# Four indirect gathers on their way at most, and weighing tile by tile, in the last three passes of a graph network

## The chip, the cores and the metric

One Trainium2 chip, and of it one core. The metric is the device time of the program in microseconds: the median of three runs. Times of single instructions, here and later, come from one execution that the hardware profiler recorded.

## The reference

Four layers of a graph network run one after the other over the same graph of 12,500 nodes with 48 features and 212,500 edges, sorted by their target node. Each layer reads the source node's row of every edge, scales it, and adds it up at the edge's target (or, in the second layer, the other way round). The third and fourth layers are what the change concerns:

```
h = relu(layernorm(x));  ex = exp(e - segment_max(e)[dst]);  a = ex / segment_sum(ex)[dst]
x = x + elu(segment_sum(h[src] * a, dst))
h = relu(layernorm(x))
y1 = segment_sum(h[src] * w, dst);  y2 = segment_sum(y1[src] * w, dst)
x = x + (h + y1 + y2) / 3
```

That makes three light passes over all edges: one for the third layer (49 columns, the last of them a column of ones that yields the sum of the weights), and two for the fourth (48 columns each).

## The kernel before

The edges are cut into tiles of 128 (one edge a partition), four tiles to a group (G = 4), eight groups to a turn of the loops (GB = 8). There are 416 groups, 52 turns and 1,664 tiles in a pass. The target nodes are cut into blocks of 128. Since the edges are sorted by target, a group touches one block or two; each block that it touches is a window.

`light_pass` (lines 718 to 822) is called three times, as `l2`, `l3a` and `l3b`, with `order` 0, 1 and 2. Its engines work so:

- **ScalarE** writes the row indices of a group as integers into a slot of `idx` (`stage`, line 743). It stages six groups ahead (LEAD = 6) of eight slots. Before it stages the group six ahead it waits for VectorE's `s_done` (line 750). Then it waits until the group's gathers have landed (line 754), and multiplies each of the four tiles by its edge weights, in place in `ring` (line 756). The fourth of these raises `s_weighed`.
- **GpSimd** waits for the group's indices (line 734) and issues four indirect gathers of 128 rows each from DRAM into `ring` (line 736). Nothing else holds it back. All four raise the group's own semaphore of eight, `s_landed_rows[j]`, by 16 each.
- **TensorE** waits for `s_weighed`, and in each window multiplies the four tiles with one-hot matrices (`hot`) and adds them up in one of two banks of `psum_acc` (line 816).
- **VectorE** makes the one-hot matrices of a window by one compare over 128 x 512 elements (line 789, two inputs in SBUF: `iota` and `dstf`). Behind it, it adds the bank of the window before to the sum of its block (`keep`, line 778). So the compare of a group's window comes behind the `keep` of the window two before it. A group's second window uses the same `hot` buffer as its first, so its compare waits until TensorE has finished the first.

The first layer (`first_pass`, its gathers in line 504) and the second (scatter-adds in line 1097) are not changed. In the second, each scatter waits on GpSimd for the scatter four before it to have landed (line 1094 to 1096, K = 4 semaphores in turn), which is the form that the change brings to the gathers.

Two semaphore habits are of use in reading the code. `sem_inc(s_seen, 1)` after a wait binds the wait to an instruction of the sequencer's own; it is one instruction with the wait. A landed DMA raises its semaphore by 16.

Of the kernel before, what the change touches and what calls it, by code (L numbers as in the profile page):

```python
# [16 lines left out]
G = 4  # L17
RING = 4
GB = 2 * RING
# [3 lines left out]
TURNS = NG // GB  # L23
# [4 lines left out]
DEPTH = GB  # L28
# [21 lines left out]
def gnn_kernel(nc, x, dst_cols, src_cols, dst_rows, src_rows, w_cols, logit_cols, logit_rows,  # L50
# [10 lines left out]
    with ExitStack() as ctx:  # L61
        def sb(name, shape, dt=f32):
            return ctx.enter_context(nc.sbuf_tensor(name, shape, dt))

        def sem(name):
            return ctx.enter_context(nc.semaphore(name))
# [41 lines left out]
        idx = sb("idx", [P, DEPTH * G], i32)  # L108
# [46 lines left out]
        ring = tbl_flat[:, 0:DEPTH * G * CS].rearrange("p (s c) -> p s c", c=CS)  # L155
# [304 lines left out]
        s_maxed = sem("s_maxed")  # L460
        s_closed = sem("s_closed")
        s_seen = sem("s_seen")
        s_landed_rows = [sem(f"s_landed_rows{j}") for j in range(DEPTH)]
        s_spread = sem("s_spread")
        s_picked = sem("s_picked")
        s_kept = sem("s_kept")
# [8 lines left out]
        def load_ranges(eng, i):  # L475

            regs = range_regs[eng]
            eng.load(regs, ranges[0:1, ds(i * (2 * GB), 2 * GB)])
            return [(eng.snap(regs[2 * j], min_val=0, max_val=NB - 1), eng.snap(regs[2 * j + 1], min_val=1, max_val=NB))
                    for j in range(GB)]  # L480
# [239 lines left out]
        def light_pass(order, name, src_table, cols, weights, total, before=None):  # L720
            s_idx = sem(name + "_idx")
            s_done = sem(name + "_done")
            s_clear = sem(name + "_clear")
            s_weighed = sem(name + "_weighed")
            s_flushed = sem(name + "_flushed")
            arrived = order * TURNS * 16 * G

            with nc.Block() as block:
                @block.gpsimd
                def _(pool):  # L730
                    with pool.Fori(0, TURNS) as i:
                        for j in range(GB):
                            pool.wait_ge(s_idx, i * GB + (j + 1))
                            pool.sem_inc(s_seen, 1)
                            for u in range(j * G, (j + 1) * G):
                                pool.indirect_dma_start(  # L736
                                    out=ring[:, u, 0:cols], out_offset=None, in_=src_table,
                                    in_offset=bass.IndirectOffsetOnAxis(ap=idx[:, u:u + 1], axis=0)).then_inc(s_landed_rows[j], 16)

                @block.scalar  # L740
                def _(act):
                    def stage(slot, column):
                        nc.scalar.copy(idx[:, slot * G:(slot + 1) * G], srow[:, ds(column, G)]).then_inc(s_idx, 1)  # L743

                    for j in range(LEAD):
                        stage(j, j * G)
                    with act.Fori(0, TURNS) as i:
                        for j in range(GB):
                            act.wait_ge(s_done, i * GB + (j + 1))
                            act.sem_inc(s_seen, 1)  # L750
                            stage((j + LEAD) % DEPTH, i * U + (j + LEAD) * G)

                            act.wait_ge(s_landed_rows[j], i * (16 * G) + (arrived + 16 * G))
                            act.sem_inc(s_seen, 1)
                            for u in range(G):
                                last = nc.scalar.activation(ring[:, j * G + u, 0:cols], ring[:, j * G + u, 0:cols], ACT.Copy,  # L756
                                                            scale=weights[:, ds(i * U + (j * G + u), 1)])
                            last.then_inc(s_weighed, 1)

                @block.vector  # L760
                def _(dve):
                    if before is not None:
                        before(dve)
                    nv.memset(acc_flat, 0.0).then_inc(s_clear, 1)
                    nv.memset(psum_acc[:, :, 0:CS], 0.0).then_inc(s_clear, 1)
                    dve.wait_ge(s_clear, 2)
                    dve.sem_inc(s_done, 1)
                    if order == 0:
                        dve.sem_inc(s_kept, 1)
                        dve.reg_mov(wn_dve, 1)  # L770
                    dve.reg_mov(before_dve, NB)

                    def keep(win, s_made):
                        k = dve.snap(before_dve, min_val=0, max_val=NB)
                        block_acc = total[:, ds(k, 1), 0:cols].rearrange("p b c -> p (b c)")
                        dve.wait_ge(s_kept, win)
                        dve.wait_ge(s_picked, win + 1)
                        nv.tensor_tensor(block_acc, block_acc,  # L778
                                         psum_acc[:, ds((win + 1) & 1, 1), 0:cols].rearrange("p r c -> p (r c)"), ALU.add).then_inc(s_made, 1)

                    with dve.Fori(0, TURNS) as i:
                        spans = load_ranges(dve, i)
                        for j in range(GB):
                            dve.reg_mov(room_dve, dve.snap(wn_dve))
                            with dve.Fori(*spans[j]) as k:
                                win = dve.snap(wn_dve)
                                dve.wait_ge(s_picked, dve.snap(room_dve))
                                dve.sem_inc(s_seen, 1)
                                nv.tensor_tensor(hot[:, j % 2, :, :],  # L789
                                                 iota[:, ds(k * P, P)].unsqueeze(1).to_broadcast([P, G, P]),  # L790
                                                 dstf[:, ds(i * U + j * G, G)].unsqueeze(2).to_broadcast([P, G, P]),
                                                 ALU.is_equal).then_inc(s_spread, 1)
                                keep(win, s_kept)
                                dve.reg_mov(before_dve, k)
                                dve.reg_add(wn_dve, wn_dve, 1)
                                dve.reg_add(room_dve, wn_dve, 1)
                            dve.sem_inc(s_done, 1)  # L797
                    keep(dve.snap(wn_dve), s_flushed)

                @block.tensor  # L800
                def _(pe):
                    if order == 0:
                        pe.sem_inc(s_picked, 2)
                        pe.reg_mov(wn_pe, 1)
                    with pe.Fori(0, TURNS) as i:
                        spans = load_ranges(pe, i)
                        for j in range(GB):
                            pe.wait_ge(s_weighed, i * GB + (j + 1))
                            pe.sem_inc(s_seen, 1)
                            with pe.Fori(*spans[j]) as k:  # L810
                                win = pe.snap(wn_pe)
                                pe.wait_ge(s_kept, win)
                                pe.sem_inc(s_seen, 1)
                                pe.wait_ge(s_spread, win)
                                for u in range(G):
                                    last = nc.tensor.matmul(psum_acc[:, ds(win & 1, 1), 0:cols].rearrange("p r c -> p (r c)"),  # L816
                                                            hot[:, j % 2, u, :], ring[:, j * G + u, 0:cols],
                                                            start=(u == 0), stop=(u == G - 1))
                                last.then_inc(s_picked, 1)
                                pe.reg_add(wn_pe, wn_pe, 1)  # L820
# [358 lines left out]


        light_pass(0, "l2", table2, CS, lg, acc)

        s_var3 = sem("s_var3"); s_std3 = sem("s_std3"); s_centred3 = sem("s_centred3"); s_squared3 = sem("s_squared3")
# [38 lines left out]
        third = 1.0 / (LAYERS + 1)  # L1222
        y1 = acc_flat[:, 0:NBW * C].rearrange("p (b c) -> p b c", c=C)
        light_pass(1, "l3a", table3[0], C, w, y1)
        s_y1out = sem("s_y1out")
        with nc.Block() as block:
# [69 lines left out]
```

## Time and profile before

| | us |
|---|---|
| median of three runs | 12057.81 |
| lowest and highest | 12056.52 and 12058.14 |
| span of the profiled execution | 14556.0 |
| GpSimd busy in that span | 9189.0 |
| TensorE matmuls busy | 6194.2 |
| VectorE busy | 4412.4 |
| ScalarE busy | 3916.7 |

The profiled execution is 2,498 us longer than the median of the runs without the profiler. Of the profiled execution no own device time is given beside its span, so the span stands for it. In the profile the light passes start at 6645.8, 9321.2 and 11919.7 us. A line of the views gives an engine, the line of the kernel, the operation, the tiles written and read, and how often it came; "idle before" is how long the engine stood still ahead of it and what ended that. DMA_INDIRECT under POOL is the time in which GpSimd makes the descriptors of a gather or a scatter, not the time in which data moves.

### The profile page before, as it was taken

The page shows a single profiled execution, that of the slowest core. Times are in us where ns is not written, and L with a number is a line of the kernel's source. Part 1 is how long each engine was busy: PE and PEld are TensorE (multiplying, and loading weights), DVE is VectorE, ACT ScalarE, POOL GpSimd, SP SyncE. Part 2 cuts the span into 40 slices and gives each one's busy share as a digit, 9 for nine tenths or more (in the row PEclk, how much of TensorE's full clock was granted, in tenths as well). Part 3 has the DMA queues.
Part 4 walks back from the last instruction along what each step waited for, and adds up shares of the span by engine and source line. Part 5 has one row for each costly group of instructions (what it writes and reads, how often), then busy time and mean ns, then how long its engine had stood idle before and what let it go on. Part 6 is the DMA issues. An engine that isn't in the chain of part 4 may idle for free. (4 is left out here: it accounts for less than half of the span.)

```text
span 14556.0 us, 229228 instructions
## 1 busy us (share of the span) xinstructions
PE 6194.2 (43%) x41742; PEld 4831.3 (33%) x41743; DVE 4412.4 (30%) x18474; ACT 3916.7 (27%) x13496; POOL 9189.0 (63%) x8348
## 2 busy tenths in 40 slices
PE   4444444444555555552333333333333333333333
PEld 2222222223444444442333333233333333333333
DVE  4444444445444444443111111211111111111111
ACT  3444444443333333321111111111121111111111
POOL 5555555556888888884666666566666656666665
DMA  4333333334455554541111111111111111111111
GB/s 116 100 102 102 99 97 96 96 94 63 61 62 61 61 62 61 62 59 42 16 16 16 16 16 16 20 16 16 16 16 16 16 21 16 16 16 16 16 16 21
DMA packets 805020, 671.18 MB, mean 46 GB/s; under 512 B 417876, under 2 KB 663828, under 8 KB 802727
## 3 DMA queue, kind: packets, MB, share of 16 engines
q0 software_dynamic: 452736, 234.14, 14.8%
q1 hardware_dynamic: 349659, 430.53, 11.2%
q10 hardware_dynamic: 2588, 6.12, 0.1%
q14 instruction: 26, 0.21, 0.0%
q8 instruction: 11, 0.18, 0.0%
HBM read 562.94 MB, written 107.13 MB: 46 GB/s over the span
## 5 line engine op out<-in xcount | busy, mean ns | idle before, releaser
L736 POOL DMA_INDIRECT table<-table,idx x4992 | 4838.7, 969 | 3149.9 <-ACT idx L743 1638.0
L816 PE MATMUL psum_acc<-table 128*128 128x48 f32 (+1 forms) x12288 | 2946.7, 417 | 5074.1 <-DVE acc L778 2363.5
L816 PEld LDWEIGHTS psum_acc<-table 128*128 128x128 f32 x12288 | 2733.0, 328 | 5287.7 <-issue 5244.2
L1097 POOL DMA_INDIRECT sums<-rows,idx x1664 | 2619.5, 1574 | 577.6 <-issue 430.9
L504 POOL DMA_INDIRECT rows<-table,idx x1668 | 1670.2, 1001 | 1581.9 <-ACT idx L556 1059.2
L789 DVE TENSOR_TENSOR table<-iota,dstf 128x512 f32 x1536 | 1064.6, 693 | 3059.2 <-issue 2074.7
L743 ACT CAST idx<-srow 128x4 int32 (+1 forms) x1266 | 243.2, 193 | 6322.7 <-DVEq L797 4262.1
L778 DVE TENSOR_TENSOR acc<-acc,psum_acc x1539 | 311.3, 202 | 3420.0 <-remote 2352.8
L704 PE MATMUL psum_acc<-parts,onehot 128*128 128x48 bf16 x6144 | 338.8, 215 | 1600.5 <-DVE onehot L647 1433.7
L1013 PE MATMUL psum_exp<-table,onet 128*128 x6144 | 432.3, 219 | 1376.2 <-DVE onet L932 1166.2
L756 ACT ACTIVATE table<-table,w 128x48 f32<-128x48 f32 x3328 | 840.6, 323 | 26.2 <-DMA table<-table,idx 12.4
L1013 PEld LDWEIGHTS psum_exp<-table,onet 128*128 128x128 bf16 x6144 | 341.8, 116 | 1510.4 <-issue 1487.5
L704 PEld LDWEIGHTS psum_acc<-parts,onehot 128*128 128x128 bf16 x6144 | 271.8, 117 | 1686.8 <-DVE onehot L647 1500.9
L986 PE MATMUL psum_mlp<-w2s,hid 49*128 49x48 f32 x3336 | 808.3, 414 | 50.8 <-DMA hid<-hid_dram 50.7
L986 PEld LDWEIGHTS psum_mlp<-w2s,hid 49*128 49x128 f32 x3336 | 741.2, 324 | 124.5 <-issue 124.5
L597 ACT ACTIVATE scratch<-drow,far 128x512 f32<-128x512 uint16 x512 | 369.3, 721 | 598.8 <-DVE segmax L666 293.2
L1064 ACT ACTIVATE gate<-psum_mlp,adapt,cw 128x48 f32<-128x48 f32 x1664 | 514.1, 390 | 48.8 <-issue 26.2
L1043 ACT CAST parts<-rest 128x196 bf16<-128x196 f32 x416 | 149.9, 360 | 1281.1 <-DVE rest L913 903.8
L964 DVE TENSOR_TENSOR idx<-srow,dmp 128x4 int32<-128x4 f32 x416 | 67.9, 163 | 1321.3 <-POOLq L1099 1243.8
L691 PE MATMUL psum_mlp<-srcrow,w1s 40*48 40x512 f32 x416 | 396.9, 1056 | 153.3 <-issue 152.2
L573 ACT ACTIVATE prod<-rows,w 128x48 f32<-128x48 f32 x1668 | 426.0, 324 | 54.0 <-issue 39.9
L756 ACT ACTIVATE table<-table,lg 128x49 f32<-128x49 f32 x1664 | 422.0, 325 | 14.2 <-DMA table<-table,idx 9.1
(183 smaller groups left out, 7162.2 us busy)
## 6 DMA issues: line engine op xcount, KB each, us to landing
drow<-rows_dram SPq DMA_DIRECT2D x832, 128.0 KB
lrow<-in_logit_rows SPq DMA_DIRECT2D x416, 256.0 KB
table<-table,idx POOLq DMA_INDIRECT x4992
srcrow<-rows_dram SPq DMA_DIRECT2D x416, 128.0 KB
hid_dram<-hid SPq DMA_DIRECT2D x416, 96.0 KB
hid<-hid_dram SPq DMA_DIRECT2D x416, 96.0 KB
rows<-table,idx POOLq DMA_INDIRECT x1668
sums<-rows,idx POOLq DMA_INDIRECT x1664
```

Of the source, the lines that this page charges most:

```text
L504: pool.indirect_dma_start(out=rows[:, u, 0:width], out_offset=None, in_=src_table, in_offset=bass.IndirectOffsetOnAxis(ap=idx[:, u:u + 1], ...
L573: last = nc.scalar.activation(prod[:, j % 2, u, 0:cols], rows[:, j % RING * G + u, 0:cols], ACT.Copy, scale=weights[:, ds(i * U + (j * G + ...
L691: nc.tensor.matmul(psum_mlp[j % 2][0:C, :], w1s[:, :], attr[j % 2], start=True, stop=True).then_inc(s_mlp1, 1)
L704: last = nc.tensor.matmul(psum_acc[:, 0, 0:cols], onehot[:, u, :], parts[:, j % 2, u, q, 0:cols], start=(u == 0 and q == 0), stop=(u == G ...
L736: pool.indirect_dma_start(out=ring[:, u, 0:cols], out_offset=None, in_=src_table, in_offset=bass.IndirectOffsetOnAxis(ap=idx[:, u:u + 1], ...
L756: last = nc.scalar.activation(ring[:, j * G + u, 0:cols], ring[:, j * G + u, 0:cols], ACT.Copy, scale=weights[:, ds(i * U + (j * G + u), 1)])
L789: nv.tensor_tensor(hot[:, j % 2, :, :], iota[:, ds(k * P, P)].unsqueeze(1).to_broadcast([P, G, P]), dstf[:, ds(i * U + j * G, G)].unsqueez ...
L816: last = nc.tensor.matmul(psum_acc[:, ds(win & 1, 1), 0:cols].rearrange("p r c -> p (r c)"), hot[:, j % 2, u, :], ring[:, j * G + u, 0:col ...
L986: last = nc.tensor.matmul(psum_mlp[j % 2][:, u * C:(u + 1) * C], hid[:, j % 2, u * P:(u + 1) * P], w2s[:, :], start=True, stop=True)
L1013: last = nc.tensor.matmul(psum_exp[j % 2][:, u * CT:(u + 1) * CT], onet[:, u * P:(u + 1) * P], table[:, ds(k, 1), q, :].rearrange("p b c - ...
L1064: last = nc.scalar.activation(gate[:, j % 2, u, 0:C], psum_mlp[j % 2][:, u * C:(u + 1) * C], ACT.Identity, scale=cw[:, ds(t, 1)], bias=ada ...
L1097: pool.indirect_dma_start(out=sums[c], out_offset=bass.IndirectOffsetOnAxis(ap=idx[:, slot:slot + 1], axis=0), in_=rows[:, slot, 0:CS], in ...
```

## The change

In the light passes there are four landing semaphores in place of eight, one for each tile of a group. GpSimd waits ahead of each gather until the gather of the same tile in the group before has landed, so that at most four gathers are on their way. In the very first turn of the first light pass the first four gathers have nothing to wait for, so that turn is written out ahead of the loop. ScalarE waits for each tile by itself instead of for the whole group.

```
-        s_landed_rows = [sem(f"s_landed_rows{j}") for j in range(DEPTH)]
+        s_landed_rows = [sem(f"s_landed_rows{u}") for u in range(G)]
...
-            arrived = order * TURNS * 16 * G
+            arrived = order * TURNS * 16 * GB
...
-                    with pool.Fori(0, TURNS) as i:
+                    def turn(i, peeled):
                         for j in range(GB):
                             pool.wait_ge(s_idx, i * GB + (j + 1))
                             pool.sem_inc(s_seen, 1)
-                            for u in range(j * G, (j + 1) * G):
+                            for u in range(G):
+                                if j > 0 or not peeled:
+                                    pool.wait_ge(s_landed_rows[u], i * (16 * GB) + (arrived + 16 * j))
+                                    pool.sem_inc(s_seen, 1)
                                 pool.indirect_dma_start(
-                                    out=ring[:, u, 0:cols], out_offset=None, in_=src_table,
-                                    in_offset=bass.IndirectOffsetOnAxis(ap=idx[:, u:u + 1], axis=0)).then_inc(s_landed_rows[j], 16)
+                                    out=ring[:, j * G + u, 0:cols], out_offset=None, in_=src_table,
+                                    in_offset=bass.IndirectOffsetOnAxis(ap=idx[:, j * G + u:j * G + u + 1], axis=0)).then_inc(s_landed_rows[u], 16)
+
+                    if order == 0:
+                        turn(0, True)
+                        with pool.Fori(1, TURNS) as i:
+                            turn(i, False)
+                    else:
+                        with pool.Fori(0, TURNS) as i:
+                            turn(i, False)
...
-                            act.wait_ge(s_landed_rows[j], i * (16 * G) + (arrived + 16 * G))
-                            act.sem_inc(s_seen, 1)
                             for u in range(G):
+                                act.wait_ge(s_landed_rows[u], i * (16 * GB) + (arrived + 16 * (j + 1)))
+                                act.sem_inc(s_seen, 1)
                                 last = nc.scalar.activation(ring[:, j * G + u, 0:cols], ring[:, j * G + u, 0:cols], ACT.Copy,
                                                             scale=weights[:, ds(i * U + (j * G + u), 1)])
                             last.then_inc(s_weighed, 1)
```

## Rows read from the trace of the kernel before

**Rows 1.** Whole execution, groups by line, engine, operation: busy, mean ns, idle before, releaser.

```profile
L736 POOL DMA_INDIRECT table<-table,idx x4992 | 4838.7, 969 | 3149.9 <-ACT idx L743 1638.0 <-issue 1511.9
L1097 POOL DMA_INDIRECT sums<-rows,idx x1664 | 2619.5, 1574 | 577.6 <-issue 430.9 <-ACT rows L1050 76.8 <-DMA sums<-rows,idx 42.6
L504 POOL DMA_INDIRECT rows<-table,idx x1668 | 1670.2, 1001 | 1581.9 <-ACT idx L556 1059.2 <-issue 522.6
```

**Rows 2.** Who waited for whom, whole execution: total us, times, longest us.

```profile
POOL table L736 <- ACT idx L743: 1638.0, 292, 103.7
```

**Rows 3.** Timeline (start, duration, engine, work): GpSimd's first gather of the later two passes.

```profile
9321.24 0.94 POOL L736 DMA_INDIRECT table<-table,idx  x1 [69.00 <-ACT idx L743]
...
11919.66 4.91 POOL L736 DMA_INDIRECT table<-table,idx  x1 [23.55 <-ACT idx L743]
```

**Rows 4.** Third light pass, groups by line.

```profile
L789 DVE TENSOR_TENSOR table<-iota,dstf 128x512 f32 x512 | 355.1, 694 | 1073.4 <-issue 746.1 <-remote 275.8 <-PE psum_acc L816 51.5
L743 ACT CAST idx<-srow 128x4 int32 x416 | 80.4, 193 | 2114.6 <-DVEq L797 1462.8 <-issue 500.2 <-remote 136.5
L756 ACT ACTIVATE table<-table,w 128x48 f32<-128x48 f32 x1664 | 420.3, 323 | 8.5 <-DMA table<-table,idx 3.3
```

**Rows 5.** Timeline: gathers one after the other.

```profile
8003.52 0.94 POOL L736 DMA_INDIRECT table<-table,idx  x1 [0.31 <-issue]
...
8012.26 0.95 POOL L736 DMA_INDIRECT table<-table,idx  x1 [0.30 <-issue]
```

**Rows 6.** Timeline at the start of the first light pass.

```profile
6649.61 0.94 POOL L736 DMA_INDIRECT table<-table,idx  x1 [0.30 <-issue]
6652.23 1.02 ACT L756 ACTIVATE table<-table,lg 128x49 f32<-128x49 f32 x4 [1.70 <-DMA table<-table,idx]
...
6657.32 1.01 ACT L756 ACTIVATE table<-table,lg 128x49 f32<-128x49 f32 x4 [3.49 <-DMA table<-table,idx]
...
6659.05 1.93 PE L816 MATMUL psum_acc<-table 128*128 128x49 f32 x8 [2.97 <-issue]
6659.70 0.95 POOL L736 DMA_INDIRECT table<-table,idx  x1 [0.30 <-issue]
...
6662.36 1.01 ACT L756 ACTIVATE table<-table,lg 128x49 f32<-128x49 f32 x4 [3.94 <-DMA table<-table,idx]
```

**Rows 7.** Timeline in the second layer: scatters, each behind a wait for an earlier one.

```profile
5002.37 1.56 POOL L1097 DMA_INDIRECT sums<-rows,idx  x1 [0.30 <-issue]
5004.23 1.56 POOL L1097 DMA_INDIRECT sums<-rows,idx  x1 [0.30 <-issue]
```

**Rows 8.** Timeline of the first light pass: compares, sums, matmuls and gathers.

```profile
8022.77 0.69 DVE L789 TENSOR_TENSOR table<-iota,dstf 128x512 f32 x1 [0.61 <-issue]
8023.38 0.20 DVE L778 TENSOR_TENSOR acc<-acc,psum_acc  x1
8023.66 0.19 ACT L743 CAST idx<-srow 128x4 int32 x1 [8.61 <-DVEq L797]
...
8023.70 3.82 PE L816 MATMUL psum_acc<-table 128*128 128x49 f32 x16 [5.99 <-DVE acc L778]
8023.85 1.01 ACT L756 ACTIVATE table<-table,lg 128x49 f32<-128x49 f32 x4
8024.16 0.69 DVE L789 TENSOR_TENSOR table<-iota,dstf 128x512 f32 x1 [0.59 <-issue]
8024.64 1.03 POOL L736 DMA_INDIRECT table<-table,idx  x1 [5.04 <-ACT idx L743]
8025.96 0.21 DVE L778 TENSOR_TENSOR acc<-acc,psum_acc  x1 [1.10 <-PE psum_acc L816]
...
8026.88 0.69 DVE L789 TENSOR_TENSOR table<-iota,dstf 128x512 f32 x1 [0.71 <-issue]
8027.22 1.17 POOL L736 DMA_INDIRECT table<-table,idx  x1 [0.30 <-issue]
8027.84 0.21 DVE L778 TENSOR_TENSOR acc<-acc,psum_acc  x1 [0.27 <-PE psum_acc L816]
```

**Rows 9.** Timeline: a compare in the middle of a gather, and one just ahead of one.

```profile
8035.01 0.94 POOL L736 DMA_INDIRECT table<-table,idx  x1 [0.30 <-issue]
8035.41 0.69 DVE L789 TENSOR_TENSOR table<-iota,dstf 128x512 f32 x1 [3.90 <-issue]
...
9154.35 0.69 DVE L789 TENSOR_TENSOR table<-iota,dstf 128x512 f32 x1 [8.62 <-issue]
9154.40 1.46 POOL L736 DMA_INDIRECT table<-table,idx  x1 [0.30 <-issue]
```

**Rows 10.** Timeline: a second window's compare behind its first window's matmuls.

```profile
7132.68 1.94 PE L816 MATMUL psum_acc<-table 128*128 128x49 f32 x8 [7.00 <-DVE table L789]
...
7134.90 0.69 DVE L789 TENSOR_TENSOR table<-iota,dstf 128x512 f32 x1 [2.35 <-PE psum_acc L816]
```

## The prediction

> **What bounds the kernel now.** I read the groups by line first [rows 1]. GpSimd does one thing in each of the three parts, and its busy time is the making of descriptors: 944 ns is the usual gather (the timeline has 0.94 almost everywhere) [rows 5], 969 ns the mean in the light passes. Between two gathers it stands still for 0.30 us, which the trace calls issue. From 8003.52 to 8012.26 there are seven gathers in 8.74 us, a period P of 1.249 us [rows 5].
>
> Then I asked how much of the profiled span is left when GpSimd never waits for indices. It waits 1,059.2 us in the first layer and 1,638.0 in the light passes [rows 1]. Of the latter, 103.7 and 69.0 and 23.6 us are the openings of the three passes, where a table is first written [rows 2, 3], and stay. 14,556.0 - 1,059.2 - 1,638.0 + 103.7 + 69.0 + 23.6 = 12,055 us. The median of the runs is 12,057.8. So I read the profiled execution as the real one plus some 2,500 us of index waits. What ends them is VectorE's late `s_done`, which VectorE's sequencer raises late (the compare and the sum idle for "issue" and "remote") [rows 4], and without the profiler this seems to be nearly absent. The real kernel then is bound by GpSimd through all its length: a light pass is 1,664 gathers x 1.249 = 2,078 us plus whatever lengthens single gathers. All terms below are worked out for such an undisturbed light pass and added to 12,058.
>
> **The wait ahead of each gather.** It adds 4,988 waits and as many small register operations on GpSimd. Queued behind each is the gather itself, and behind that all further gathers and the next group's index wait; ScalarE waits for them. Two things must be known. First, when it is met: ScalarE starts to weigh 2.62 and 2.66 us after the start of the group's last gather [rows 6], its own start-up within. The gather four later starts at 4 P = 5.00 us. Second, how much ahead GpSimd must be released: after the end of an index write it needs 24.64 - 23.85 = 0.79 us to start a gather [rows 8]. 5.00 - 2.66 - 0.79 leaves 1.55 us. So the limit of four is never reached: at the start of a gather two or three are on their way. The nearest row for the same form is the scatter, with a wait ahead of each: the gap stays 0.30 [rows 7]. There the wait for an earlier scatter does end 42.6 us of idle time in 1,664 [rows 1]; for 4,992 gathers that would be 128 us, the upper bound. Below zero nothing can come of it, since nothing competes for what fewer gathers would free. I take 0, nearest to the 0.30 row, and the 1.55 us is the cover: if landing took 4.2 us in place of 2.66, each further 0.1 us would cost 0.1 us a group, 125 us in all. The turn that is written out once costs nothing I can name.
>
> **The waits of ScalarE.** Three more waits and value computations a group. The present one costs nothing visible: index write until 23.85, weighing from 23.85 [rows 8]. ScalarE has 0.19 + 1.01 us of work in a group of 5.00 us. At 0 to 0.1 us each, they are hidden, all but that of the fourth tile, which was there before as the group's.
>
> **What tile by tile moves.** Tiles 0 to 2 are weighed while later ones are being gathered. Behind the last landing stands one multiply of 0.33 us instead of four in 1.01 us. Everything behind it, TensorE and VectorE, comes 0.68 us earlier against GpSimd's beat. At the end of a pass that is a gain of 0.68 us, 2 us for three. In the middle no one waits for it. It has a side effect, though, and this is what I rest the forecast on.
>
> **The compare holds up the gather.** A gather that starts while a compare runs takes longer. Compare 9154.35, gather 9154.40: 1.46 us instead of 0.94. Compare 0.34 us ahead: 1.17. Compare 0.48 us ahead: 1.03. A compare that starts 0.40 us into a gather: 0.94 [rows 8, 9]. All lie on one line: the gather is longer by 0.565 us less the compare's lead, for leads from about 0.05 to 0.565, and otherwise not at all. The sum (line 778), with one of its two inputs in PSUM, shows no such effect. 126 us of the light passes' 4,838.7 are of this kind (4,838.7 - 4,992 x 0.944), 8 of them two gathers at the third pass's opening, the first of 4.91 us [rows 3].
>
> The Trainium skill (SBUF — State Buffer, Who interferes with whom) says that a two-input VectorE instruction takes the read side of a shared port pair against GpSimd, and infers that this leaves descriptor making alone. The rows say otherwise, at least for the read of the indices at its start. By the page's inference the side effect would be nil and the time 12,056.
>
> So the question is where the compares fall in the beat. With s the start of a group's last gather:
> - A regular compare: 2.66 to the weighing, 1.01 the four multiplies, 0.72 to the first matmul (6658.33 to 6659.05) [rows 6], 1.93 the matmuls, 0.32 to the sum (8027.52 to 8027.84) and 0.92 from sum to compare (8025.96 to 8026.88) [rows 8]: s + 7.56. The sixth gather after s starts at 7.49. The compare comes 0.07 after it: harmless. With the change: s + 6.88, between the fifth (6.24) and the sixth, 0.61 ahead of this: harmless, by 0.05 us.
> - A pass has 512 compares for 416 groups [rows 4], so 96 groups have a second window (taken as two at most). Its compare waits for the first window's matmuls: 0.28 us here [rows 10], 0.32 to the sum [rows 8]; I take 0.36, with the register operations that the sum lacks. s + 6.68; before, 0.44 after the fifth gather, harmless. With the change s + 6.00, 0.24 ahead of it: 0.32 us.
> - The compare behind it follows at 1.39 (8022.77 to 8024.16). Before: 8.07, 0.58 after the sixth, harmless. Changed: 7.39, and the sixth now starts at 7.49 + 0.32, a lead of 0.42: 0.14 us.
> - The third follows the second window's matmuls: 0.92 + 1.93 + 0.32 + 0.92 = 4.09 after the first. Before: 10.77, a lead of 0.47 on the ninth gather at 11.24: 0.10 us. Changed: 10.09, lead 0.36 on the eighth at 9.99 + 0.46: 0.20 us.
>
> Before 0.10, changed 0.66 us, for 96 groups and three passes: 29 and 190 us, a difference of 161.
>
> These leads hang on hundredths. The whole chain may be shorter or longer without the profiler by an unknown e, the same for both kernels. At e = -0.1 and +0.1 the same arithmetic gives about 165 and 180. At -0.2 the regular compares of before lead by 0.13 and cost some 0.17 us each (a delay pushes the next lead down, so less than half of the 0.43 remains), and the difference falls to about 23. At +0.2 the second-window compare of the changed kernel no longer leads, and the changed kernel gains some 48. Landings scatter too and smear this. The mean of these five is 96; less 2 for the pass ends that is 94, and the forecast is 12,058 + 94 = 12,152 us, 0.8% slower.
>
> **The rivals.**
> - No measurable change. The phases smear out so that both kernels pay alike, or the queue of ready gathers hides what the compare takes. For it: ScalarE, TensorE and VectorE are off the bound, and the limit does not bind. Against it: the gather is the bound, so that each lengthening counts in full. Time 12,056.
> - Faster. The place is the same, the fifth to ninth gather after a landing, and the price the same, but before pays: if the real chain is 0.2 us or more longer, or 0.15 to 0.4 shorter with little damping, its compares lead and the changed ones do not. It decides at a regular lead above 0.05 us before. For it: 12,055 above includes the traced 126 us of such lengthening, room for before to be paying. Against: most of those in the trace follow a restart of GpSimd after an index wait (8024.64), which the real run lacks. Gain 48 to 126: about 11,985.
> - The landing wait binds after all: 128 us by the scatter's row, 12,186.
>
> **How the numbers follow.** Forecast 0.42, no change 0.25, faster 0.27, landing wait 0.06. What can be told from no change is about 0.2%, 24 us. Slower than that: 0.46 (a little of the forecast's own spread falls below 24); within: 0.27; faster: 0.27. The forecast's own range is 12,080 to 12,250 (23 to 192 more). To 8 in 10 it must take in no change and the nearer part of faster: 12,000 to 12,250.
>
> **What would show it.** In the changed profile: 0.30 us ahead of gathers and no "DMA" among the releasers of line 736's successor (the wait is never late); single multiplies in step with the gathers at a pass start, and the first matmul about 0.7 us sooner after the last landing; the mean gather above 969 ns if the forecast holds, and many gathers of 1.1 to 1.3 us in undisturbed stretches. I am wrong if an effect stays with the group-wise wait of ScalarE restored, or if removing the second input's conflict from the compare changes nothing.

## The result, and the profile after

The changed kernel takes 12,187.5 us (median of four runs, 12,185.2 to 12,189.7) against 12,057.2 before: 130 us more, ratio 1.0108 with a 95% interval of 1.0094 to 1.0123. The forecast was 12,152 us, with a range of 12,000 to 12,250.

The profiled execution of the changed kernel has a span of 12,183.5 us, as long as its runs. That of before had 14,556.0 and was 2,500 us too long. So its trace is no fair partner, and the kernel before was profiled again (label `r1_before_again`, below): span 12,053.8, as long as its runs. From here on "before" in comparisons is that trace.

GpSimd's groups by line, with busy time, mean ns of one, and idle time ahead and its releasers, first of the changed kernel, then of the kernel before in its new trace. They answer to [rows 1]. "Gaps" below means the idle time between two gathers.

```profile
L739 POOL DMA_INDIRECT table<-table,idx x4992 | 4898.2, 981 | 1732.1 <-DMA table<-table,idx 1299.1 <-issue 253.5 <-ACT idx L754 179.6
L1108 POOL DMA_INDIRECT sums<-rows,idx x1664 | 2620.9, 1575 | 577.8 <-issue 434.6 <-ACT rows L1061 73.5 <-DMA sums<-rows,idx 44.1
L504 POOL DMA_INDIRECT rows<-table,idx x1668 | 1697.2, 1018 | 546.5 <-issue 474.6 <-ACT idx L556 71.8
```

```profile
L736 POOL DMA_INDIRECT table<-table,idx x4992 | 4804.7, 962 | 1699.4 <-issue 1511.5 <-ACT idx L743 187.9
L1097 POOL DMA_INDIRECT sums<-rows,idx x1664 | 2621.4, 1575 | 577.1 <-issue 442.1 <-ACT rows L1050 72.9 <-DMA sums<-rows,idx 36.5
L504 POOL DMA_INDIRECT rows<-table,idx x1668 | 1693.6, 1015 | 546.5 <-issue 478.8 <-ACT idx L556 67.7
```

The whole difference of the spans, 129.7 us, is in these rows. The gathers of the light passes take 4,898.2 - 4,804.7 = 93.5 us more, the gaps between them 1,732.1 - 1,699.4 = 32.7 more, the first layer's gathers (unchanged code) 3.6 more, the scatters 0.2. The index waits of the old trace (1,059.2 and 1,638.0 in [rows 1]) are 67.7 and 187.9 here, most of the latter the openings of the passes.

One name misleads. The changed kernel's 1,299.1 us "DMA" are 4,264 gaps of 0.30 us, the ordinary gap that is called "issue" before: where a gather has a wait ahead of it, the profile names the wait's releaser for the gap, even when it was met long before.

The longer gathers are seen in a timeline of the changed kernel, around a group with a second window (start, duration, engine, work):

```profile
8003.63 0.94 POOL L739 DMA_INDIRECT table<-table,idx  x1 [0.30 <-issue]
8004.57 0.69 DVE L800 TENSOR_TENSOR table<-iota,dstf 128x512 f32 x1 [4.86 <-PE psum_acc L827]
8004.88 1.20 POOL L739 DMA_INDIRECT table<-table,idx  x1 [0.30 <-DMA table<-table,idx]
...
8005.96 0.69 DVE L800 TENSOR_TENSOR table<-iota,dstf 128x512 f32 x1 [0.59 <-issue]
8006.38 1.09 POOL L739 DMA_INDIRECT table<-table,idx  x1 [0.30 <-DMA table<-table,idx]
...
8008.68 0.69 DVE L800 TENSOR_TENSOR table<-iota,dstf 128x512 f32 x1 [0.72 <-issue]
8009.02 1.17 POOL L739 DMA_INDIRECT table<-table,idx  x1 [0.30 <-DMA table<-table,idx]
```

Three compares lead a gather by 0.31, 0.42 and 0.34 us, and the gathers are 0.26, 0.15 and 0.23 us longer than 0.94: each 0.565 less the lead. The same place before, again with the compares of a second window and of the group behind it:

```profile
8001.94 0.94 POOL L736 DMA_INDIRECT table<-table,idx  x1 [0.30 <-issue]
8002.26 0.69 DVE L789 TENSOR_TENSOR table<-iota,dstf 128x512 f32 x1 [4.76 <-PE psum_acc L816]
...
8003.19 0.94 POOL L736 DMA_INDIRECT table<-table,idx  x1 [0.30 <-issue]
...
8003.66 0.69 DVE L789 TENSOR_TENSOR table<-iota,dstf 128x512 f32 x1 [0.59 <-issue]
8004.43 0.94 POOL L736 DMA_INDIRECT table<-table,idx  x1 [0.30 <-issue]
...
8013.10 0.69 DVE L789 TENSOR_TENSOR table<-iota,dstf 128x512 f32 x1 [0.72 <-issue]
8013.17 1.45 POOL L736 DMA_INDIRECT table<-table,idx  x1 [0.30 <-issue]
```

The first two compares start 0.32 and 0.47 us after a gather's start and cost nothing. But the last pair shows what before does pay: a regular compare (one of a group's first window) which comes 0.07 us ahead of a gather, and costs 0.51.

The longer gaps stand ahead of every 110th gather of the changed kernel, 45 times, 0.8 to 1.25 us instead of 0.30:

```profile
5783.19 0.94 POOL L739 DMA_INDIRECT table<-table,idx  x1 [0.31 <-issue]
5785.09 0.95 POOL L739 DMA_INDIRECT table<-table,idx  x1 [0.95 <-issue]
...
5925.56 0.95 POOL L739 DMA_INDIRECT table<-table,idx  x1 [0.30 <-issue]
5927.70 0.94 POOL L739 DMA_INDIRECT table<-table,idx  x1 [1.19 <-issue]
```

### The profile page after: what moved, and what is told of

It reads as the page before. It is cut to its first block and busy times, and to the rows that moved or that the text cites. A ratio compares the mean times of both kernels' runs of the same rounds, so it can differ in the third digit from the quotient of the medians.

```text
span 12183.5 us, 240282 instructions
## 1 busy us (share of the span) xinstructions
PE 6218.6 (51%) x41742; PEld 4831.6 (40%) x41743; DVE 4451.5 (37%) x18474; ACT 4143.7 (34%) x13496; POOL 9277.1 (76%) x8348
## 5 line engine op out<-in xcount | busy, mean ns | idle before, releaser
L739 POOL DMA_INDIRECT table<-table,idx x4992 | 4898.2, 981 | 1732.1 <-DMA table<-table,idx 1299.1
L504 POOL DMA_INDIRECT rows<-table,idx x1668 | 1697.2, 1018 | 546.5 <-issue 474.6
L767 ACT ACTIVATE table<-table,w 128x48 f32<-128x48 f32 x3328 | 1050.0, 332 | 2055.8 <-DMA table<-table,idx 2030.0
L767 ACT ACTIVATE table<-table,lg 128x49 f32<-128x49 f32 x1664 | 526.9, 333 | 1028.0 <-DMA table<-table,idx 1015.1
```

The source lines that it names most:

```text
L504: pool.indirect_dma_start(out=rows[:, u, 0:width], out_offset=None, in_=src_table, in_offset=bass.IndirectOffsetOnAxis(ap=idx[:, u:u + 1], ...
L739: pool.indirect_dma_start(out=ring[:, j * G + u, 0:cols], out_offset=None, in_=src_table, in_offset=bass.IndirectOffsetOnAxis(ap=idx[:, j ...
```

## Experiments

The theory: waiting tile by tile moves VectorE's compares into the way of the gathers. The rivals: the limit of four, or the waits themselves, cost the time, and no VectorE instruction matters. Where a ratio is given, it is against the kernel before.

**The kernel before once more, for its profile.** No edit.

> The kernel before, unchanged, to get a profile of it that is as long as its runs. The profile that the prediction rests on was 2,498 us longer than the runs; that of the changed kernel is not. Theory (compares hold up gathers): span near 12,056; the light-pass gathers take in sum 4,712 us plus 30 to 60 (mean 950 to 956 ns) against 4,898 (mean 981) in the changed kernel, so that their difference alone gives 130 us. Rival (landing wait): the gathers sum to the same 4,898 and the difference stands in the gaps between them.

Measured: 12,057.4 us, ratio 0.9998 (0.9987 to 1.0008), gathers 4,804.7 us, mean 962. The direction is as the theory has it, but the gathers of before are longer by 93 us than 4,712, not by 30 to 60. Their difference gives 94 of the 130 us, not all. The other 33 are in the gaps: so both the theory and a rival have a part.

**Limit of four, ScalarE waits for the whole group.**

```
                             for u in range(G):
                                 act.wait_ge(s_landed_rows[u], i * (16 * GB) + (arrived + 16 * (j + 1)))
                                 act.sem_inc(s_seen, 1)
+                            for u in range(G):
                                 last = nc.scalar.activation(...)
```

> The changed kernel with its limit of four gathers and its wait ahead of each on GpSimd, but ScalarE waits for all four tiles before it weighs the first. Theory (tile by tile moves the compares by 0.68 us into the gathers' path): back to the kernel before, 12,057, ratio 1.000 within 0.002. Rival (landing wait or the added instructions on GpSimd): stays at 12,187, ratio 1.011.

Measured: 12,099.9 us, ratio 1.0034 (1.0022 to 1.0047). Two thirds of the loss go, one third stays. The prediction had named this as a sign of being wrong: "an effect stays with the group-wise wait of ScalarE restored". One does, 43 us. The gathers are back, the gaps are not:

```profile
L739 POOL DMA_INDIRECT table<-table,idx x4992 | 4810.9, 964 | 1735.2 <-DMA table<-table,idx 1294.2 <-ACT idx L754 290.7 <-issue 150.3
```

**Limit of eight, tile by tile.**

```
-        s_landed_rows = [sem(f"s_landed_rows{u}") for u in range(G)]
+        s_landed_rows = [sem(f"s_landed_rows{u}") for u in range(2 * G)]
...
-            arrived = order * TURNS * 16 * GB
+            arrived = order * TURNS * 16 * (GB // 2)
...
-                                if j > 0 or not peeled:
-                                    pool.wait_ge(s_landed_rows[u], i * (16 * GB) + (arrived + 16 * j))
+                                v = j % 2 * G + u
+                                if j > 1 or not peeled:
+                                    pool.wait_ge(s_landed_rows[v], i * (8 * GB) + (arrived + 16 * (j // 2)))
```

(and `v` in the gather and in ScalarE's wait likewise)

> The changed kernel with eight landing semaphores and a limit of eight gathers; ScalarE still waits tile by tile. Theory: as the changed kernel, 12,187, ratio 1.011. Rival (a limit of four is tight): back towards 12,057.

Measured: 12,131.9 us, ratio 1.0062 (1.0045 to 1.0079). Neither expectation is met: the limit is worth some 55 us against the changed kernel by the medians, 43 by the spans of the two profiled executions, and 33 by their gaps. The gaps are back, the gathers are not:

```profile
L740 POOL DMA_INDIRECT table<-table,idx x4992 | 4889.4, 979 | 1699.0 <-DMA table<-table,idx 1378.2 <-ACT idx L755 178.8 <-issue 142.0
```

**The changed kernel with another compare.**

```
-                                nv.tensor_tensor(hot[:, j % 2, :, :],
-                                                 iota[:, ds(k * P, P)].unsqueeze(1).to_broadcast([P, G, P]),
-                                                 dstf[:, ds(i * U + j * G, G)].unsqueeze(2).to_broadcast([P, G, P]),
-                                                 ALU.is_equal).then_inc(s_spread, 1)
+                                for u in range(G):
+                                    spread_hot = nv.tensor_scalar(hot[:, j % 2, u, :], iota[:, ds(k * P, P)],
+                                                                  dstf[:, ds(i * U + (j * G + u), 1)], None, ALU.is_equal)
+                                spread_hot.then_inc(s_spread, 1)
```

> The changed kernel with the one-hot compare as four instructions over 128x128 with one SBUF matrix and a scalar column each, in place of one with two SBUF matrices over 128x512. Theory, if the second matrix input is what holds up the gather: all of the 178 us that gathers are longer goes, 12,187 - 178 = about 12,010, below the kernel before, and the light-pass gathers have a mean near 945 ns. Rival 1 (any VectorE instruction that reads SBUF holds it up): stays at 12,100 to 12,200. Rival 2 (landing wait): stays at 12,187 with a mean of 981 ns unchanged or lower but the time not.

Measured: 12,020.9 us, ratio 0.9969 (0.9956 to 0.9981), 166 us below the changed kernel though VectorE works longer: its four instructions cover 0.93 and 1.02 us in the timeline where one took 0.69. The gathers have a mean of 948 ns, and one that a compare leads by 0.77 us while its four parts still run is not longer:

```profile
8002.64 1.02 DVE L801 TENSOR_SCALAR table<-iota,dstf 128x128 f32 x4 [0.73 <-issue]
8003.41 0.94 POOL L739 DMA_INDIRECT table<-table,idx  x1 [0.30 <-DMA table<-table,idx]
```

```profile
L739 POOL DMA_INDIRECT table<-table,idx x4992 | 4732.5, 948 | 1735.6 <-DMA table<-table,idx 1443.9 <-ACT idx L754 185.5 <-issue 106.2
```

So it is the compare in its old form that holds up the gather, and no other VectorE work in these passes does so to speak of. The edit changes two things at once, the second matrix input and the size (four of 128x128 in place of one of 128x512). That the second input is what counts is the likelier reading, since each of the four parts still runs 0.3 us beside the gathers, but no run separates the two.

**Limit of eight, ScalarE waits for the group.** The two edits of above together.

> Limit of eight gathers with a wait ahead of each on GpSimd, ScalarE waits for the whole group. So far the kernel with a limit of four and group waits took 12,100, and its trace has a gap of about 1.0 us instead of 0.30 ahead of every 110th gather, which the limit of eight with tile waits does not have. Theory (the added waits cost nothing; the limit of four exposes a pause of GpSimd's sequencer): 12,057, ratio 1.000 within 0.002, sum of gathers about 4,805. Rival (waits ahead of each gather cost by themselves, whatever the limit): about 12,100.

Measured: 12,060.9 us, ratio 1.0001 (0.9991 to 1.0010). A wait ahead of each gather is free by itself, to within 0.1%.

```profile
L740 POOL DMA_INDIRECT table<-table,idx x4992 | 4810.5, 964 | 1699.8 <-DMA table<-table,idx 1298.2 <-ACT idx L755 273.3 <-issue 128.3
```

**Limit of eight, tile by tile, and a delay.**

```
                                 act.sem_inc(s_seen, 1)
+                                if u == G - 1:
+                                    for _ in range(9):
+                                        act.sem_inc(s_delay, 1)
```

> Limit of eight, ScalarE waits tile by tile, but nine semaphore increments on ScalarE between the last tile's wait and its multiply, some 0.68 us, the time by which tile by tile is earlier. Theory (only the moment of the compares against the gathers counts): falls from 12,132 back to about 12,060 although ScalarE has more to do. Rival (tile-wise waits cost by themselves, on ScalarE or through semaphore traffic): 12,132 or more.

Measured: 12,065.3 us, ratio 1.0005 (0.9995 to 1.0014); without the delay it was 1.0062. The delay puts the last tile's weighing 0.60 us later (median), and this extra work for ScalarE makes the kernel 67 us faster, since the compares fall about where they were before. They lengthen the gathers by 94 us here, by 163 without the delay:

```profile
L741 POOL DMA_INDIRECT table<-table,idx x4992 | 4812.1, 964 | 1699.6 <-DMA table<-table,idx 1314.1 <-ACT idx L756 258.5 <-issue 127.1
```

**The kernel before with the other compare**, in the light passes (the edit above, on the kernel before):

> The kernel before (no limit, group waits), with the light passes' compare as four instructions with one SBUF matrix and a scalar column. Theory: the 97 us by which its gathers are longer than 944 ns fall to about 25, as in the changed kernel with these compares, and nothing else moves: 12,057 - 72 = 11,985, ratio 0.994. Rival (the gain in the changed kernel came from elsewhere): 12,057.

Measured: 11,987.8 us, ratio 0.9942 (0.9929 to 0.9956), as expected.

```profile
L736 POOL DMA_INDIRECT table<-table,idx x4992 | 4733.9, 948 | 1699.4 <-issue 1520.0 <-ACT idx L743 179.3
```

**And in the first layer too.**

```
-                                nv.tensor_tensor(onehot[:, :, :], iota[:, ds(k * P, P)].unsqueeze(1).to_broadcast([P, G, P]),
-                                                 dstf[:, ds(i * U + j * G, G)].unsqueeze(2).to_broadcast([P, G, P]),
-                                                 ALU.is_equal).then_inc(s_hot, 1)
+                                for u in range(G):
+                                    first_hot = nv.tensor_scalar(onehot[:, u, :], iota[:, ds(k * P, P)],
+                                                                 dstf[:, ds(i * U + (j * G + u), 1)], None, ALU.is_equal)
+                                first_hot.then_inc(s_hot, 1)
```

> As before, and the same compare in the first layer too, whose 1,668 gathers have a mean of 1,015 ns, 118 us over 944 each. VectorE is busy there for most of the time, and four instructions take some 1.0 us instead of 0.69. Theory, if that compare is half of what holds up these gathers and VectorE keeps up: 11,985 - 40 to 70 = about 11,930. Rival (VectorE becomes the bound in the first layer): 12,000 or more.

Measured: 11,942.8 us, ratio 0.9904 (0.9889 to 0.9919): 114 us below before by the medians of other runs of it, 117 by those beside it, 245 below the changed kernel, and within what was expected. The first layer's gathers fall from a mean of 1,015 to 995 ns, 28% of their excess over 944. Other VectorE instructions there have two matrix inputs too and may be behind the rest, which was not tested.

```profile
L504 POOL DMA_INDIRECT rows<-table,idx x1668 | 1660.3, 995 | 547.1 <-issue 473.0 <-ACT idx L556 74.0
```

**What the pause goes by.** Limit of four, group waits, and `pool.sem_inc(s_delay, 1)` ahead of every gather.

> Limit of four, group waits on ScalarE, and one semaphore increment more on GpSimd ahead of every gather. The kernel without it takes 12,100 and has a gap of 0.8 to 1.25 us ahead of every 110th gather, 45 in all. Theory A (the pause of GpSimd's sequencer belongs to its stream of instructions): the distance between such gaps changes from 110, to about 80 with a fifth to a quarter more instructions, and with them the time, to about 12,115. Theory B (it belongs to the number of gathers): the distance stays 110 and the time 12,100. Either way the increment itself costs nothing: gaps of 0.30 us elsewhere.

Measured: 12,104.2 us, ratio 1.0036 (1.0017 to 1.0056). The distance stays 110 gathers, and the gaps are 45 in number as before, which is theory B: the pause goes with the number of gathers, not with that of instructions.

```profile
L741 POOL DMA_INDIRECT table<-table,idx x4992 | 4809.0, 963 | 1738.3 <-DMA table<-table,idx 1304.2 <-ACT idx L756 281.9 <-issue 152.2
```

The parts together, in us; "gathers" and "gaps" are GpSimd's busy and idle time of the light passes' line:

| kernel | time | ratio | gathers | gaps |
|---|---|---|---|---|
| before | 12,057 | | 4,804.7 | 1,699.4 |
| limit 8, group | 12,061 | 1.0001 | 4,810.5 | 1,699.8 |
| limit 8, tile, delay | 12,065 | 1.0005 | 4,812.1 | 1,699.6 |
| limit 4, group | 12,100 | 1.0034 | 4,810.9 | 1,735.2 |
| limit 8, tile | 12,132 | 1.0062 | 4,889.4 | 1,699.0 |
| limit 4, tile (the change) | 12,187 | 1.0108 | 4,898.2 | 1,732.1 |

Tile by tile costs 79 to 87 us in gathers at either limit, the limit of four 33 to 35 us in gaps with either wait. The two add up in these sums; of the ratios, 0.34% and 0.62% make 0.96% where 1.08% was measured, a difference within their intervals.

## Why the prediction was right, and where it was not

**GpSimd bounds the kernel: right.** What the kernels differ by in its gathers and gaps is found again in the spans of their profiled executions, to within 9 us.

**The old trace as the real run plus index waits: right in the main, to the microsecond by luck.** The sum of 12,055 us was drawn from it; the new trace's span is 12,053.8. But the same working by parts makes the light passes 43 us longer than in the new trace and the first layer 47 us shorter, and the two cancel.

**The compare holds up the gather, by 0.565 us less its lead: right.** Summed over all compares of the changed kernel's trace with leads of 0.045 to 0.565 us, that line gives 176 us, and the gathers that follow are longer by 177. In the new trace of before both are 87. With the other compare the lengthening goes. Here the Trainium skill (SBUF — State Buffer, Who interferes with whom) infers that such an instruction leaves descriptor making alone; the runs say otherwise, up to 0.52 us a gather, and the measurement decides. Its rule that the order of issue decides who blocks is borne out by the trace in both directions. A compare that starts at least 0.045 us ahead of a gather goes first, and the gather is longer. One that starts from 0.045 us ahead to 0.02 us behind is itself the one that is held up: 129 of the 1,536 compares before take 0.70 to 0.77 us instead of 0.69, all end 0.72 us after the gather's start, and the gather keeps its 0.94:

```profile
5979.69 0.94 POOL L736 DMA_INDIRECT table<-table,idx  x1 [0.30 <-issue]
5979.70 0.72 DVE L789 TENSOR_TENSOR table<-iota,dstf 128x512 f32 x1 [0.71 <-issue]
...
8073.56 0.77 DVE L789 TENSOR_TENSOR table<-iota,dstf 128x512 f32 x1 [0.72 <-issue]
8073.61 0.94 POOL L736 DMA_INDIRECT table<-table,idx  x1 [0.30 <-issue]
```

A compare that starts later within a gather takes its 0.69 us, and the gather its 0.94. So in these traces the two collide about a gather's start only, not over all of its 0.94 us.

**How much earlier tile by tile makes the chain: right.** From a group's last gather to its first matmul the prediction had 4.39 us before and 3.71 with the change. The medians are 4.33 and 3.71, so 0.62 us in place of 0.68.

**Where the compares fall: right for the changed kernel, off for before.** The table sets the traces against the prediction. Each cell has the lead over the next gather in us (predicted, or the measured median; "none" is a lead above 0.565), then the cost in us summed over the three passes. There are 288 compares of each of the first three kinds.

| compare | predicted lead, cost before | measured | predicted lead, cost changed | measured |
|---|---|---|---|---|
| second window's | none, 0 | none, 0 | 0.24, 92 | 0.29, 79 |
| the one behind | none, 0 | none (0.73), 5 | 0.42, 40 | 0.42, 37 |
| the third | 0.47, 29 | 0.53, 15 | 0.36, 58 | 0.35, 46 |
| all others | 0.07 behind, 0 | about the gather's start, 67 | 0.61, 0 | 0.65 to 0.69, 15 |

The first three rows are the step that carried the forecast: 161 us predicted, 141 measured. The last row failed: the prediction had the regular compare 0.07 us after a gather's start in before and called it harmless. In the real run the chain is 0.06 us shorter than the slowed trace had it, the median of these compares is 0.01 us after a gather's start, and the chain scatters, from 4.25 to 4.47 us between its tenth and its ninetieth percentile. Of the compares four groups behind a second window, 44% come 0.045 to 0.565 us ahead of a gather, most of them by less than 0.3, where the price is highest, and they alone make 48 us. In all, before pays 67 us that the prediction did not charge, against 15 in the changed kernel: a term mis-sized by some 50 us. The spread over the unknown e, which took 161 down to 96, made up for it: 93.5 us were measured. That it came so near is in part luck, since the mean of five values of e stood in for a size that the prediction did not know.

**The wait ahead of each gather costs nothing, "the 1.55 us is the cover": this step failed.** The waits are free, but a limit of four is not: 33 us. The prediction says that "the limit of four is never reached". GpSimd's sequencer, which runs ahead of the making of descriptors, reaches it at nearly every gather. In the changed kernel the record of the wait stands 0.02 us behind the landing of the gather four before, at 1,223 of the 1,247 gathers for which the trace tells that landing. The landings do not come late. From the start of a gather to its landing it is

```profile
DMA to landing us min/median/max: 2.3/2.4/6.2
```

and so the wait ends 2.59 us (median) ahead of the start of its own gather. A gather starts as little as 0.78 us after its wait, so that in the ordinary case nothing is lost, as predicted. What was left out is what the sequencer itself does now and then. Once in 110 gathers it leaves no record for 3.2 us, and the gather just ahead of this pause starts 3.43 us after its wait, the same in all 45 cases. That is 0.84 us more than the 2.59, and a gap of 0.5 to 0.95 us beyond the usual 0.30 opens, 34 us in all. With a limit of eight the waits end 7.6 us ahead, and the same pause (3.1 us, then once in 106 gathers) leaves no gap. The scatter's row, used as the upper bound (128 us), covered the cost, but it was read as landing waits, and those 42.6 us are the ordinary 0.30 gaps under another name (140 times, 0.3 each). So the bound was wide enough, but not for the reason given.

**ScalarE's own waits are hidden: right.** The delay experiment adds nine instructions to each group at no cost (12,065 us against 12,061 for the group-wise wait at the same limit).

So 12,152 against 12,187 is near for reasons partly other than those given: the collisions came out as the mean of the five cases had it (93.5 us against 96), and the pause, which the sum had at nothing, is nearly all of the rest (33). Of the two signs of being wrong that the prediction named, one came true (an effect of 43 us stays with the group-wise wait) and one did not (another compare does take the time away). The test named for the landing wait, no "DMA" among the releasers, was a bad one; the sum of the gaps was the right one.

## What to carry to other kernels

Where GpSimd makes descriptors without a break, a VectorE compare of two SBUF matrices (128x512 here) that starts up to half a microsecond ahead of a gather lengthens it. How many do so is a matter of how the rhythms of the two engines fall together. An edit that only makes an engine earlier which is not the bottleneck can cost time, and a useless delay can gain some. Take the conflict away (a column as scalar operand in place of the second matrix) rather than tune the rhythm. A limit on transfers in flight has to leave the issuing engine room for its own pauses, not for the transfers' latency alone; compare the sums of busy and idle time, since the named releaser of a gap may have been met long before.

## What the runs showed of the hardware that was not expected

- GpSimd's sequencer is silent for 3.2 us once in 110 gathers of 128 rows at a limit of four, for 3.1 us once in 106 at a limit of eight; one more instruction ahead of each gather leaves the 110 as it is. In both cases distance and limit add up to 114. What it does then stays open, and whether it pauses so without a limit can't be read from the trace, where it has too few records.
- A gather's start is sensitive for a moment only. A compare that starts after it does no harm, and one 0.07 us before it costs 0.51; one that starts less than 0.045 us before it costs the gather nothing and is itself held up, to 0.77 us.
- GpSimd's sequencer runs ahead of the making of descriptors as far as the limit lets it, by 2.6 us at four and 7.6 us at eight, so its waits for landings are nearly always waited for in earnest, though they cost nothing in the ordinary case.
- One profiled execution of the kernel before was 2,500 us longer than its runs and than a second one; in it VectorE's register and semaphore instructions took 0.7 us each in stretches of the light passes, against 0.02 to 0.24 in the second. Why is open. The sum of busy time and minimal gaps of the bound engine gave the real time all the same.
